# A four-layer image kernel: new orders of steps on every engine, small norm and extremes operations rewritten, the latest producer awaited first

## What is computed

```
x = x + L0(gn(x))   # vector quantiser: nearest of 1024 codes by |f|^2 + |e|^2 - 2 f.e; the code's vector is added
x = x + L1(gn(x))   # f, g: 32 wide, h: 256 wide; sigmoid(f_i . g_j) over the 64 positions of an image row, times h
x = x + L2(gn(x))   # x0, x1, x2 = three columns; sm = softmax over n of x0[n] * x1[m]; gate = sigmoid(x2 @ sm); gate * input
x = x + L3(gn(x))   # q, k, v of 4 heads x 32; softmax(q) over d, softmax(k) over the 4096 positions;
                    # context = k v; out = q context; projection to 256; layer norm with gamma and beta
```

## Time and profile before

| | us |
|---|---|
| median of 3 runs | 5449.4 (5445.9 to 5449.4) |
| profiled execution | 5439.4 |
| its span | 5437.6 |

### The profile page before, as it was taken

One profiled execution on the slowest core, in us unless ns is written; L12 is line 12 of the kernel. 1 busy time (PEld: TensorE's weight loads), 2 busy tenths in 40 slices (PEclk: granted clock), 3 DMA queues, 4 the chain that ended last, 5 costly groups with the idle time before them and its releaser, 6 DMA issues.

```text
span 5437.6 us, 109580 instructions
## 1 busy us (share of the span) xinstructions
PE 5072.3 (93%) x42984; PEld 2685.9 (49%) x42984; DVE 4387.4 (81%) x9218; ACT 4036.2 (74%) x6279; POOL 1966.0 (36%) x1594
## 2 busy tenths in 40 slices
PE   7799999999999999999999999999999999999986
PEld 3436445363553645446464553645446464453624
DVE  8478787887878888797887978888798887978836
ACT  1477878778786877868778786787868778786795
POOL 4225143352523425243351523425244351433403
PEclk9899999999999999999999999999999999999998
DMA  2010201102021020211102021020211102011000
GB/s 75 26 41 12 76 27 55 43 6 81 21 71 32 21 69 15 74 29 44 51 9 79 24 66 36 21 67 17 71 32 39 55 11 77 25 61 39 13 32 32
DMA packets 167965, 227.84 MB, mean 42 GB/s; under 512 B 13792, under 2 KB 146656, under 8 KB 167456
## 3 DMA queue, kind: packets, MB, share of 16 engines
q1 hardware_dynamic: 142880, 153.70, 8.5%
q0 software_dynamic: 24576, 67.14, 4.3%
HBM read 153.55 MB, written 67.24 MB: 41 GB/s over the span
## 4 chain that ended last, share of the span: by engine, by line
PE 71%; DVE 13%; ACT 10%; issue 4%; POOL 1%; DMA 0%; DVEq 0%; SPq 0%; ACTq 0%; POOLq 0%
PE PS L1239 37%; PE PS L1416 12%; PE PS L1407 5%; PE PS L1350 3%; PE PS L1515 2%; ACT big L618 2%; PE PS L1273 2%; ACT n_x L551 2%; DVE work L896 2%; PE PS L1297 2%; DVE stats L878 2%; ACT soft L618 1%; PE PS L1316 1%; DVE idx L902 1%; PE PS L1365 1%
## 5 line engine op out<-in xcount | busy, mean ns | idle before, releaser
L618 ACT ACTIVATE big<-PS 128x1024 f32<-128x1024 f32 x1216 | 1207.3, 1028 | 361.2 <-PE PS L1407 327.1
L441 POOL DMA_INDIRECT quant_H<-emb_t,idx x512 | 510.5, 997 | 905.0 <-DVE idx L902 878.4
L1239 PE MATMUL PS<-e_hi,n_hi 128*128 128x512 f16 x2048 | 780.0, 381 | 17.8 <-DVE m L896 10.1
L1239 PE MATMUL PS<-e_lo,n_hi 128*128 128x512 f16 x2048 | 776.7, 379 | 0.0
L1239 PE MATMUL PS<-e_hi,n_lo 128*128 128x512 f16 x2048 | 776.7, 379 | 0.0
L618 ACT ACTIVATE soft<-PS 128x1024 f32<-128x1024 f32 x576 | 577.5, 1030 | 254.3 <-PE PS L1407 244.8
L878 DVE BATCH_NORM_STATS2 stats<-XT 128x6 f32<-128x512 f32 x1024 | 652.9, 683 | 11.0 <-POOL XT L454 1.0
L1416 PE MATMUL PS<-big,w 128*4 128x512 f32 x4864 | 652.6, 622 | 0.0
L902 DVE FIND_INDEX8 idx<-m,work 128x8 uint32<-128x1024 f32 x512 | 624.4, 1220 | 0.0
L1407 PE MATMUL PS<-rhs,lhs 32*128 32x512 bf16 x3584 | 514.7, 395 | 80.3 <-ACT big L618 41.9
L495 POOL TENSOR_TENSOR rstd<-rstd,mhalf 128x4 f32<-128x4 f32 x128 | 132.0, 1031 | 1114.9 <-DVE rstd L1091 1114.9
(11 more groups left out here) (214 smaller groups left out, 11014.2 us busy)
## 6 DMA issues: line engine op xcount, KB each, us to landing
xin<-x SPq DMA_DIRECT2D x128, 512.0 KB, 4.3
out<-yout SPq DMA_DIRECT2D x128, 512.0 KB, 3.1
o_both<-rows_d SPq DMA_DIRECT2D x32, 512.0 KB, 7.1
quant_H<-emb_t,idx POOLq DMA_INDIRECT x512
XT<-emb SPq DMA_DIRECT2D x1, 1024.0 KB, 6.0
rows_d<-n_hi SPq DMA_DIRECT2D x32, 4.0 KB
XT<-wh SPq DMA_DIRECT2D x1, 256.0 KB, 5.6
XT<-wqv SPq DMA_DIRECT2D x1, 256.0 KB, 5.6
```

Source lines behind the costliest of these rows:

```text
L441: nc.gpsimd.indirect_dma_start(quant[:, g % 2, u, :], None, emb_t, bass.IndirectOffsetOnAxis(ap=idx[:, t % (2 * GT), 0:1], axis=0),).then_ ...
L618: nc.scalar.activation(E[h % 3][:, z * 1024:(z + 1) * 1024], bank(2 * z, 2), ACT.Exp).then_inc(exped.sem, 1)
L1239: ins = mm(dst, a, b, start=first and j == 0, stop=last and j == 2)
```

## The change

Three things change; the arithmetic results are the same functions of the same data.

1. **Order.** The lists of steps of the loop pass and of the epilogue are written anew on PE, DVE, ACT and SP, in the loop pass on POOL too; the steps are the same ones. In the pass 82 of 402 steps on PE stand elsewhere, 75 of 294 on DVE, 40 of 254 on ACT, 6 of 78 on POOL, 5 of 16 on SP, by at most 11, 20, 7, 1 and 3 places.
2. **Small operations.** In `gn` the variance becomes one operation per channel half with both operands as per-partition scalars, instead of a product and a sum over both halves; the shift likewise. In `extremes` the first product goes to PSUM (`above`), so the maximum reads one operand from SBUF and one from PSUM.
3. **Waits.** In steps with several waits the one for the producer that comes last is written first. `score` waits for the low half once in four tiles.

The diff, cut to its core:

```diff
@@ SP, loop pass
-                exp(old, 0, 0); rows_back(old); final_out(last, 1); final_out(last, 3); turn_in(new, 1)
-                turn_in(new, 3); final_out(last, 5); turn_in(new, 5); turn_in(new, 7); final_out(last, 7)
...
+                rows_back(old); exp(old, 0, 0); turn_in(new, 1); final_out(last, 1); final_out(last, 3)
+                final_out(last, 5); final_out(last, 7); turn_in(new, 3); turn_in(new, 5); final_out(last, 9)
...
@@ ACT, l0_norm (l1_norm, l3_norm and l3_qv likewise)
                 if k == 0:
+                    act.wait_ge(*l0_xn.after(im, g))
                     act.wait_ge(*l0_scored.room(im, 2 * (g * GT + GT) - 1, 4 * GT))
-                    act.wait_ge(*l0_xn.after(im, g))
@@ DVE, gn
                     link(v.tensor_tensor(dm[:, q, :], dm[:, q, :], PS[:, b, 0:KC], ALU.subtract))
-                    link(v.tensor_tensor(vv[:, q, :], dm[:, q, :], dm[:, q, :], ALU.mult))
-                    v.tensor_tensor(vv[:, q, :], vv[:, q, :], mv[:, q, :, 1], ALU.add).then_inc(var_ready[layer].sem, 1)
+                    for k in range(KC):
+                        last = v.tensor_scalar(vv[:, q, k:k + 1], dm[:, q, k:k + 1], dm[:, q, k:k + 1], mv[:, q, k, 1:2],
+                                               ALU.mult, ALU.add)
+                    last.then_inc(var_ready[layer].sem, 1)
...
-                    v.scalar_tensor_tensor(out=gt[:, layer, :], in0=gm[:, q, :], scalar=-1.0, in1=gs[:, layer, :], op0=ALU.mult,
-                                           op1=ALU.mult).then_inc(gn_ready[layer].sem, 1)
+                    for k in range(KC):
+                        last = v.tensor_scalar(gt[:, layer, k:k + 1], gm[:, q, k:k + 1], gs[:, layer, k:k + 1], -1.0,
+                                               ALU.mult, ALU.mult)
+                    last.then_inc(gn_ready[layer].sem, 1)
@@ DVE, best
                 if half == 0:
+                    dve.wait_ge(*l0_scored.after(im, 2 * t))
                     dve.wait_ge(*l0_indexed.room(im, t, 2))
                 else:
                     dve.wait_ge(*l0_maxed.after(im, 2 * t))
-                dve.wait_ge(*l0_scored.after(im, 2 * t + half))
+                    dve.wait_ge(*l0_scored.after(im, 2 * t + 1))
@@ DVE, extremes
-                v.tensor_scalar(ma[:, 0, :], s3[:, 1, :], mx2[:, 0:1], None, ALU.mult)
-                link(v.tensor_scalar(ma[:, 1, :], s3[:, 1, :], mx2[:, 1:2], -1.0, ALU.mult, ALU.mult))
-                link(v.tensor_tensor(s3[:, 2, :], ma[:, 0, :], ma[:, 1, :], ALU.max))
+                above = PS[:, 7, 264:264 + NT]
+                v.tensor_scalar(above, s3[:, 1, :], mx2[:, 0:1], None, ALU.mult)
+                link(v.tensor_scalar(ma[:, :], s3[:, 1, :], mx2[:, 1:2], -1.0, ALU.mult, ALU.mult))
+                link(v.tensor_tensor(s3[:, 2, :], ma[:, :], above, ALU.max))
@@ DVE, l3_qsoft_ (gating, l3_q, final_sq and final_out likewise)
+                dve.wait_ge(*l3_qrec.after(im, g))
                 dve.wait_ge(*l3_qturned.room(im, g, 2))
-                dve.wait_ge(*l3_qrec.after(im, g))
@@ PE, score
+                if half == 0 and t % GT == 0:
+                    pe.wait_ge(*l0_lo.after(im, g))
                 pe.wait_ge(*l0_maxed.room(im, 2 * t + half, 2))
-                if half == 0:
...
-                    pe.wait_ge(*l0_lo.after(im, g))
@@ PE, turn0 (l1_fg, l1_h, l3_k and l3_qv: the producer's wait ahead of the room's)
-                pe.wait_ge(*l0_added.room(im, p, 1))
...
                     pe.wait_ge(gathered[g % 2][u], 16 * (n + 1))
+                    if c == 0:
+                        pe.wait_ge(*l0_added.room(im, p, 1))
```

597 lines of the change are left out of this document (298 added, 299 removed).

## The result

The changed kernel takes 5399.0 us (median of 4 runs, 5383.6 to 5403.8) against 5447.9 of the kernel before measured beside it (5445.9 to 5449.4). The ratio is 0.9909, with a 95% interval of 0.9898 to 0.9921: about 49 us saved, where 23 were forecast. The profiled execution took 5400.9 us, its span is 5399.0.

A forecast was written before the change was run, and what follows sets the result against it. PE, busy 93% of the span, was taken to set the pace. Waits -20 and -2, port -9, small operations +8 and order 0 sum to -23, from 5449.4 to 5426 us; range 5393 to 5466.

The forecast's parts named there:

- Parts 1 and 2: Steps with several waits: last producer's wait on the instruction, -20 us; 384 fewer PE waits in the score matmuls, -2.
- B: The code scores' stage of one image's period: PE busy 127.97 of 132.80 us; to shorten by about 0.5 us.
- C: Layers 1 and 3 of one image's period: PE busy 99.80 of 105.90 us; to shorten by about 0.5 us.
- stage A: Final steps of one image, transposes and exponentials of the next: ACT comes first, busy 87.55 of 90.80 us.
- part 1: Wait order on DVE and ACT: 58 us of engine time saved, a third reaching the end, -20 us.
- Part 3: Norm variance and extremes on DVE, held by POOL's split: new forms free the variance step, -9 us.
- part 5: New orders of steps on the engines: no row signs their effect, 0 us (-30 to +30).
- Part 4: More small operations in the norm: variance +0.03 us, shift +0.23, over 64 norms; +8 us of at most 16.6.
- Rival 3: SP's queue: first store late behind the fourth load, delaying DVE's output step, up to 42 us; 5468 us, chance 0.16.
- Rival 2: Across DVE, PE and ACT: waits give 45 us, port 17, small operations cost 8; 5395 us, chance 0.17.
- What is late next is stage A: After the change, ACT stays within 3.3 us of that stage's length whatever else happens.

The follow-up runs named there:

- e1: The kernel before with only the order of the waits changed; 5424.3 us, ratio 0.9964.
- e4: The kernel before with the new step orders and small operations, the waits as before; 5424.8 us, ratio 0.9962.
- e2: The kernel before with only the new orders of steps; 5411.0 us, ratio 0.9934.
- e5: The kernel before with the new orders and waits, the small operations as before; 5384.1 us, ratio 0.9888.
- e3: The kernel before with only the small operations of norm and extremes changed; 5449.3 us, ratio 1.0010.
- e17: The changed kernel with the norm's old operations, the extremes as changed; 5382.1 us, ratio 0.9889.
- e13: The kernel before with new orders and waits, but old small operations and SP's old loop-pass order; 5368.1 us, ratio 0.9862.
- e14: As e13, with the extremes as one product to PSUM and one fused operation that takes the maximum; 5356.4 us, ratio 0.9840.
- e7: The kernel before with the new step order only in layers 1 and 3 of the loop pass; 5441.6 us, ratio 0.9995.

## Why the prediction was right and wrong

- **Parts 1 and 2, the waits: right in size, wrong in place.** -22 forecast, -21 measured alone (e1), 26 to 27 on top of the new orders (e4 to changed, e2 to e5). The latencies of the earlier trace rows came down as priced, 0.14 to 0.03 and 107 to 34 ns. But a third of every stage's latency did not arrive: nearly nothing in B and C and most of it in stage A, where I had thought ACT's own work to be the limit. That the total came out within 1 us is luck in part. The wait that gave up its place paid a little: the output step now starts 0.09 us behind POOL's `rstd` where it started 0.035 behind, 44 times in e1, 2.4 us, near the 3 that I had taken off. The Trainium skill ("VectorE: DVE Perf Modes", The DRAIN you can't avoid), by which part 1 would be worth nothing, speaks of semaphores set by each copy; a second wait, which stands here as an instruction of its own, is another thing, and the 13.7 us before L1017 fell to 4.4 when its two waits changed places.
- **Part 3, the port: the mechanism and the -9 were right on the old orders** (stage C of e3), and so was the second product that is held in the first one's stead. The step that failed is that I took each part against the kernel before: part 5's own listing shows the variance step moved ahead of the key copy, out of POOL's way, and with it part 3 has nothing to save (C is 1007.1 us in e2, 1008.1 in e4).
- **Part 4: the sum of the price was right (0.26 forecast, 0.27 measured) by luck, the share about right.** The halves were off in opposite directions (+0.03 and +0.23 forecast, +0.10 and +0.17 measured). I took half, 8 us; the stages of the changed kernel show 9, in full in B, 0.22 of 0.27 in A, and 0.12 of 0.54 in C, where other images' steps do cover the norms of layers 2 and 3. The medians say 11 to 17 (e5 and e17); what is beyond 9 goes with a lower clock, a term the sum did not have, and its cause stays open.
- **Part 5, the orders at 0: the error.** This is the step that put the forecast at less than half of what came. The term was -35, of which SP's queue takes +16 to +23, so the rest of the lists is worth some -55 (e13 against e1, each by its saving: -56). I had "no row that signs the rest" and put in 0 with a half-width of 30. The earlier trace rows had a sign to offer: in stage A ACT was idle for 3.3 us and PE for 4.5, so neither filled the stage and each waited for the other; a range of 30 us with its middle at 0 said nothing of that. What the runs show in its place is ACT's wait for PE's products in stage A: 3.3 us a pass before, 2.8 with the waits alone, 1.3 in the changed kernel, 0.6 with SP's old order.
- **Rival 3 was no rival but a part of the sum.** The queue was read rightly, and its price (0 to 42) covers the measured 16 to 23; the late transfer was another, the fifth load behind four stores, not the first store. I compared its time with one use of the buffer only. And since it was held as a case with a chance of 0.16 instead of a term, the forecast lacked it; had the rest of the orders been priced rightly, its absence would have cost some 20 us of error in the other direction.
- **Rival 2's time (5395) is the nearest, by another road.** It let nearly all of the waits' latency arrive (45 of 58) and the port give 17. Neither happened.
- **"What is late next is stage A" was half right.** ACT limits it, but at 88.4 us (e14), not at 90.8; the space was in the order.

## What to carry to other kernels

Put the wait that ends last on the instruction itself: it costs next to nothing (2.4 us here) and gave 0.4%. Before a remedy for a collision is kept, see whether a new order has already taken the two apart: the remedy's own price (0.27 us a norm, 9 us or more in all) stays. See also which step the new order puts in the old one's place: here the query step took over a part of the hold. And on a queue that only issues transfers, follow every transfer that comes behind a moved one to its reader, loads as well as stores.

## What was unexpected of the hardware

- PE's granted clock fell to half for 3.4 or 6.8 us at a time, mostly in three places of a pass (and for longer in prologue and epilogue): at the start of stage A, and before the first steps that follow the norms of layers 0 and 1. A drop of 3.4 us ahead of the first best step costs nothing visible (in the changed kernel A was 89.4 and 89.6 us with it and without it), one at the start of A mostly 1.3 us or more, one before `l1_h` 0 to 2 us. Runs of one kernel differ by 20 us and more (the changed one 5384 to 5404, e7 5432 to 5453), and the fastest of the changed one, 5383.6, had a granted clock of 0.981 against 0.976. Over 85 runs of the kernel before, 0.001 of granted clock goes with 1.9 us.
- A vector operation of one element per partition takes 270 ns with two per-partition scalars (variance) or 209 ns with one and a constant (shift), where 160 ns do for two elements without per-partition scalars. They overlap only a little: two take 0.46 and 0.33 us.
- Vector operations from SBUF to SBUF on 32 elements were held by POOL's split for 1.1 to 1.3 us in every run that had them beside it, products to PSUM beside it were not (254 ns), and the 128x512 query step took 1.07 instead of 0.69 us; of the one-element forms of the variance 30 begin under a split in e3, and the longest took 274 ns. Of the rule that the prediction cites (the Trainium skill, "Advanced Engine Details and Errata", VectorE Performance Modes) both halves agree here: 32 elements from SBUF to SBUF wait (1412 ns), one element does not (274 ns at most).
